# The last convolution units combined one median sooner, and four of sixteen final sums moved from VectorE to TensorE

## The chip, the cores and the metric

One core of a Trainium2 chip runs the kernel; the metric is its device time in microseconds, as the median of several executions. The engines are TensorE (PE, matrix products; its weight loads are PEld), VectorE (DVE), ScalarE (ACT), GpSimd (POOL) and SyncE (SP), which here issues every transfer.

## The reference

The input is 16 images of 128 channels by 32x32 pixels, float32. Only the end of the computation is touched by the change:

```python
y = conv3x3(concat([rimg0, rimg1], axis=1), convW_w) + convW_b      # 256 -> 128 channels
x = relu(batchnorm(y, bnW_gamma, bnW_beta))                         # statistics over all 16 images
m = median_blur(x, 3)                                               # 3x3 median, zero padding
out = x + einsum('bchw,oc->bohw', m, W) + b                         # W: 128x128
```

`rimg0` and `rimg1` come from Haar wavelet transforms of the input, the first through a 1x1 convolution, a batch norm and a ReLU (BN1). The second batch norm (BN3 in the code) needs sums over all images, so nothing of `x` exists before the last image of `y` does. Scaling by a positive factor and ReLU keep an order, so the kernel takes the medians of `y` itself, and applies scale, shift and ReLU to the median afterwards.

## The kernel before, in words

Channels lie on the 128 partitions. The 3x3 convolution runs over 20 units (`UNITS`): each image is one unit, except images 0, 1, 14 and 15, which are two units of half the rows. Units 16 and 17 are image 14, units 18 and 19 image 15. A unit u uses one of two PSUM buffers, `conv_ps[:, u % 2]`, of two banks. TensorE makes its products P and Q there (`pq`, lines 398 to 410); ScalarE copies P out (`keep_p`, line 562); VectorE puts P+Q and P-Q into the banks (`seed_even`, `seed_odd`, lines 745 to 757); TensorE adds the other taps (`outputs`, line 412); ScalarE copies the result to `y` and sums it and its squares (`keep_y`, lines 564 to 576).

TensorE's program is `outputs(u-2)`, `pq(u)`, one unit after the other, and last `outputs(19)`. `outputs(u)` waits for `seeded`, which VectorE gives when it has combined P and Q of u.

VectorE's program is one list of median pieces (`PIECES`, one for each unit; `median`, line 759), 18 instructions each. Inside the piece of unit u it combines unit u+2: early, behind line 827, or late, around line 842. The pieces of units 18 and 19 run through `step_and_more`, which counts instructions and puts others between them: BN3's fifteen small ones behind the 8th (`BN3_AT`), and one `finish(n)` behind each of the 15th to 28th (`FINISH_AT`).

Once BN3 is there, the last stage runs. ScalarE applies scale, shift and ReLU to the median of each image (`norm_median`, line 618). GpSimd zeroes its corner pixels (line 349) and maps `y` to scale*y + shift + bias (`map_x1`, line 340) for three images of four, ScalarE for the fourth (line 621). TensorE multiplies the median by W (`mix`, line 463) into `conv_ps[:, n % 2]`, and waits for `finish(n-2)`, since that reads the same buffer. VectorE's `finish(n)` (line 914) forms out = max(mapped, bias) + mix in one instruction, and SyncE sends it. Image 15 is finished and sent in two halves. Between the convolution and the mixes TensorE runs 24 products of zeros (`KEEP_WARM`, line 477).

Of the kernel before, what the change touches and what calls it, by code (L numbers as in the profile page):

```python
# [5 lines left out]
def wavelet_conv_median_kernel(nc, x, w1_t, w3_t, w2_t, vectors, out):  # L6
# [26 lines left out]
    LOW = -1.0e30  # L33
    PAIRS = IMAGES // 2
    R_HALF, X_HALF = 0, 1
    WARM_UP, KEEP_WARM = 8, 24
    RING = 8


# [25 lines left out]
    with ctx:  # L65
        def sb(name, shape, dt=fp32):
            return ctx.enter_context(nc.sbuf_tensor(name, shape, dt))
# [23 lines left out]
        v1 = sb("v1", [CH, 2 * KY * CH])  # L91
        w1 = sb("w1", [CH, CH])
        w2 = sb("w2", [CH, CH])
        p_kept = [sb(f"p_kept{k}", [CH, BANK]) for k in range(2)]
        sorted_cols = sb("sorted_cols", [CH, 3 * COLS])
        col_lo, col_mid, col_hi = (sorted_cols[:, k * COLS:(k + 1) * COLS] for k in range(3))
# [84 lines left out]
        warm = sem("warm")  # L181
        med_ready = sem("med_ready")
        mix_done = sem("mix_done")
        out_ready = sem("out_ready")
        out_sent = sem("out_sent")

# [4 lines left out]
        def zslot(n):  # L191
            return z[:, n, :]
# [31 lines left out]
        @block.sync  # L224
        def _(sp):
            sp.dma_start(w1[:, :], w1_t).then_inc(w1_in, 16)
            w3_cols = w3_t.rearrange("c t o -> c (t o)")
            for n in range(RING):
                sp.dma_start(ring[n][:, :], x_img[:, n, :]).then_inc(x_in[n], 16)
            sp.dma_start(vec[:, :], vectors).then_inc(vec_in, 16)  # L230
            for half in (X_HALF, R_HALF):
                cols = slice(half * KY * KX * CH, (half + 1) * KY * KX * CH)
                sp.dma_start(wt[:, cols], w3_cols[:, cols]).then_inc(w3_in[half], 16)
            for n in range(RING, IMAGES):
                sp.wait_ge(x_in[n - RING], 16)
                wait_xu12(sp, n - RING)
                sp.dma_start(ring[n - RING][:, :], x_img[:, n, :]).then_inc(x_in[n - RING], 16)
            sp.dma_start(w2[:, :], w2_t).then_inc(w2_in, 16)

            for n in range(IMAGES):  # L240
                if n < 2:
                    sp.wait_ge(x_in[n], 32)
                    wait_xu12(sp, n + RING)
                else:
                    sp.wait_ge(raw_in[n % 2], 16 * (n // 2))
                    sp.wait_ge(xu03_made, n - 1)
                    sp.wait_ge(x_edges_made, n - 1)
                sp.dma_start(raw[n % 2][:, :], x_img[:, n, :]).then_inc(raw_in[n % 2], 16)
            for n in range(IMAGES - 1):
                sp.wait_ge(out_ready, n + 1)  # L250
                sp.dma_start(out_img[:, n, :], slot(n)).then_inc(out_sent, 16)
            for part in range(2):
                sp.wait_ge(out_ready, IMAGES + part)
                half = slice(part * HALF, (part + 1) * HALF)
                sp.dma_start(out_img[:, IMAGES - 1, half], slot(IMAGES - 1)[:, half]).then_inc(out_sent, 16)
            sp.wait_ge(out_sent, 16 * (IMAGES + 1))

        @block.gpsimd
        def _(pool):
# [68 lines left out]
            for n in range(2, IMAGES):  # L328
# [18 lines left out]
            for n in range(1, IMAGES):  # L347
                pool.wait_ge(med_normed, n)
                G.memset(at(zslot(n), 0, [[(H - 1) * W, 2], [W - 1, 2]]), 0.0).then_inc(med_ready, 1)  # L349
                if n % 4 < 4 - ACT_SHARE:  # L350
                    map_x1(n)

        @block.tensor
        def _(pe):
# [121 lines left out]
            for _ in range(KEEP_WARM):  # L476
                nc.tensor.matmul(conv_ps[:, other, 0:BANK], zeros[:, 0:CH], zeros[:, :], start=True, stop=True)
            pe.wait_ge(w2_in, 16)
            pe.wait_ge(squares_summed, PARTS_ALL)
            for n in range(2):  # L480
                mix(n, n)
            for n in range(2, IMAGES):
                pe.wait_ge(out_ready, n - 1)
                mix(n, n % 2)

        @block.scalar
        def _(act):
# [132 lines left out]
            def map_x1(n):  # L620
                S.activation(slot(n), slot(n), ACT.Identity, bias=shift3_bias2[:, :], scale=scale3[:, :]).then_inc(x1_by_act, 1)

            for n in range(1, 4):
                norm_median(n)
            for n in range(4 - ACT_SHARE, 4):
                map_x1(n)
            for n in range(4, IMAGES):
                norm_median(n)
                if n % 4 >= 4 - ACT_SHARE:
                    map_x1(n)  # L630

        @block.vector
        def _(dve):
# [125 lines left out]
            def median(n, kept, pair0=0, pairs=BH, step=step, seeds=None):  # L759

                early, late = (seeds, None) if n in HALVED or n + 2 in HALVED else (None, seeds)
# [92 lines left out]
                PIECES.append((n, done_pairs, upto - done_pairs, u))  # L854
                done_pairs = upto

            def medians(pieces, step=step, seeds=None):
                for n, pair0, pairs, u in pieces:
                    ins = median(n, 2 * (u + 1), pair0, pairs, step, seeds)
# [13 lines left out]
            dve.wait_ge(pads_set, 1)  # L873

            dve.wait_ge(pre_kept, len(PRE))
            for u in range(len(UNITS) - 2):
                medians(PIECES[u:u + 1], seeds=u + 2)

            def second_batch_norm():
                dve.wait_ge(squares_summed, PARTS_ALL)  # L880
# [23 lines left out]
                V.scalar_tensor_tensor(shift3_bias2[:, :], mid3[:, :], neg_scale3[:, :], beta_bias2[:, :], ALU.mult, ALU.add).then_inc(bn3_ready, 1)  # L904

            def finish(n, first=0, count=PIX, part=0):
                g, k = divmod(n, 4)
                if k >= 4 - ACT_SHARE:
                    dve.wait_ge(x1_by_act, g * ACT_SHARE + k + 1 - (4 - ACT_SHARE))
                else:  # L910
                    dve.wait_ge(x1_by_pool, g * (4 - ACT_SHARE) + k + 1)
# [5 lines left out]
            for n, instruction in enumerate(FINISH_AT):  # L917
                place[instruction] = lambda n=n: finish(n)
            done = [0]

# [10 lines left out]
            for n in range(len(FINISH_AT), IMAGES - 1):  # L931
# [31 lines left out]
```

## Time and profile before

| | us |
|---|---|
| median of 3 runs (lowest, highest) | 419.66 (417.89, 421.17) |
| profiled execution, its own time | 418.86 |
| its span, first to last instruction | 417.1 |
| TensorE busy | 396.9 (95%) |
| VectorE busy | 375.6 (90%) |
| ScalarE / GpSimd busy | 152.9 / 190.8 |
| mean granted TensorE clock | 0.98 of full speed |

The span is the time between the first and the last instruction of the profiled execution; its own time has 1.76 us more around it. Starts in the rows below are counted from the start of the span. A row's length is that of the instruction, and neighbours on one engine overlap by some hundredths of a microsecond.

### The profile page before, as it was taken

What the parts mean: (1) busy time and instruction counts of PE and PEld (TensorE: products, weight loads), DVE (VectorE), ACT (ScalarE), POOL (GpSimd) and SP (SyncE); (2) the same over time, 40 slices, a digit from 0 to 9 for tenths busy, and PEclk for the clock granted to TensorE, in tenths of its full rate; (3) what the DMA queues carried; (4) which work ended last, traced back from release to release, by engine and by line L of the source; (5) the groups of instructions that cost most, each with busy time, mean ns of one, the idle gap of its engine ahead of it and who ended that gap; (6) DMA issues with size and microseconds to landing.
All of it is one profiled execution on the core that took longest, in us unless ns stands there. A gap on an engine that the chain in (4) does not pass through costs nothing.

```text
span 417.1 us, 3651 instructions
## 1 busy us (share of the span) xinstructions
PE 396.9 (95%) x1120; PEld 210.5 (50%) x1120; DVE 375.6 (90%) x532; ACT 152.9 (37%) x348; POOL 190.8 (46%) x194
## 2 busy tenths in 40 slices
PE   7889999999999999999999999999999998699983
PEld 2335588856444444444444444444446787564331
DVE  3899857999849999999999998989989999999993
ACT  2565753412262432323241414141424222229902
POOL 3999395622624443445454343434343520006620
PEclk9999999999999999999999999999999999889995
DMA  8970200100101011010101001010100000002673
GB/s 301 410 320 3 95 6 2 50 0 2 51 0 50 4 47 52 0 50 0 50 2 51 27 23 50 3 50 0 51 0 2 0 1 2 0 0 116 282 282 127
DMA packets 7796, 26.72 MB, mean 64 GB/s; under 512 B 992, under 2 KB 1248, under 8 KB 7776
## 3 DMA queue, kind: packets, MB, share of 16 engines
q1 hardware_dynamic: 7776, 26.48, 16.7%
q8 instruction: 9, 0.15, 0.1%
q14 instruction: 11, 0.09, 0.1%
HBM read 18.09 MB, written 8.39 MB: 63 GB/s over the span
## 4 chain that ended last, share of the span: by engine, by line
PE 71%; DVE 13%; POOL 5%; ACT 5%; issue 3%; DMA 2%; SPq 0%; POOLq 0%; DVEq 0%
PE conv_ps L381 65%; ACT z L618 3%; PE one_ps L363 3%; PE one_ps L446 2%; POOL y L212 2%; POOL y L213 2%; DMA ru<-x 2%; PE conv_ps L469 1%; POOL y L340 1%; DVE one_ps L821 1%; DVE sorted_cols L792 1%; DVE sorted_cols L794 1%; DVE sorted_cols L790 1%; DVE sorted_cols L787 1%; DVE z L823 1%
## 5 line engine op out<-in xcount | busy, mean ns | idle before, releaser
L381 PE MATMUL conv_ps<-ru,wt 128*128 128x512 f32 (+1 forms) x360 | 133.7, 509 | 0.0
L381 PEld LDWEIGHTS conv_ps<-ru,wt 128*128 128x128 f32 x360 | 69.9, 195 | 53.9 <-issue 50.2
L381 PE MATMUL conv_ps<-xu,wt 128*128 128x496 f32 (+3 forms) x240 | 88.6, 506 | 5.6 <-DVE conv_ps L757 5.6
L569 ACT ACTIVATE y<-conv_ps,sgn 128x512 f32<-128x512 f32 (+1 forms) x40 | 25.5, 637 | 171.0 <-PE conv_ps L381 171.0
L381 PEld LDWEIGHTS conv_ps<-xu,wt 128*128 128x128 f32 x240 | 46.0, 193 | 42.0 <-issue 33.2
L319 POOL TENSOR_TENSOR ru<-eo 128x512 f32<-128x512 f32 x16 | 17.0, 1061 | 86.5 <-DVE one_ps L785 86.4
L219 POOL TENSOR_TENSOR ru<-z 128x512 f32<-128x512 f32 x14 | 18.1, 1290 | 59.4 <-DVE one_ps L827 59.4
L381 PE MATMUL conv_ps<-ru,v 128*128 128x496 f32 (+3 forms) x120 | 43.7, 500 | 0.0
L381 PE MATMUL conv_ps<-y,wt 128*128 128x496 f32 (+3 forms) x108 | 38.6, 491 | 0.0
L381 PE MATMUL conv_ps<-y,v 128*128 128x496 f32 (+3 forms) x108 | 38.6, 491 | 0.0
L469 PE MATMUL conv_ps<-z,w 128*128 128x512 f32 x64 | 31.2, 637 | 4.8 <-POOL z L349 4.3
L363 PE MATMUL one_ps<-y,w 128*128 128x512 f32 x64 | 30.4, 605 | 4.9 <-DVE z L661 2.6
L533 ACT ACTIVATE z<-z,bn 128x256 f32<-128x256 f32 x64 | 33.0, 589 | 1.2 <-DVE bn L726 1.2
L381 PEld LDWEIGHTS conv_ps<-ru,v 128*128 128x128 f32 x120 | 22.8, 190 | 18.0 <-issue 16.8
L381 PEld LDWEIGHTS conv_ps<-y,v 128*128 128x128 f32 x108 | 20.5, 190 | 16.2 <-issue 15.3
L381 PEld LDWEIGHTS conv_ps<-y,wt 128*128 128x128 f32 x108 | 20.5, 190 | 16.2 <-issue 15.3
L562 ACT ACTIVATE p_kept<-conv_ps 128x512 f32<-128x512 f32 (+1 forms) x20 | 10.2, 512 | 48.0 <-PE conv_ps L381 48.0
L784 DVE TENSOR_TENSOR one_ps<-y 128x512 f32<-128x512 f32 (+2 forms) x20 | 11.8, 588 | 17.3 <-ACT y L569 17.3
L575 ACT ACTIVATE conv_ps<-conv_ps,neg_shift,sgn 128x512 f32<-128x512 f32 (+1 forms) x40 | 26.3, 657 | 0.0
L311 POOL TENSOR_TENSOR eo<-ru 128x512 f32<-128x512 f32 x16 | 20.7, 1292 | 8.3 <-DVE ru L741 7.1
L914 DVE SCALAR_TENSOR_TENSOR y<-y,vec,conv_ps 128x1024 f32<-128x1024 f32 (+1 forms) x17 | 20.6, 1211 | 3.9 <-PE conv_ps L469 3.9
L469 PEld LDWEIGHTS conv_ps<-z,w 128*128 128x128 f32 x64 | 11.6, 197 | 23.2 <-DVE y L914 14.1
(128 smaller groups left out, 639.8 us busy)
## 6 DMA issues: line engine op xcount, KB each, us to landing
raw<-x SPq DMA_DIRECT2D x20, 512.0 KB, 3.3
out<-y SPq DMA_DIRECT2D x15, 512.0 KB, 2.6
ru<-x SPq DMA_DIRECT2D x8, 512.0 KB, 8.7
xu<-x SPq DMA_DIRECT2D x4, 512.0 KB, 8.7
wt<-w_t SPq DMA_DIRECT2D x2, 576.0 KB, 10.6
out<-y SPq DMA_DIRECT2D x2, 256.0 KB, 2.1
w<-w_t SPq DMA_DIRECT2D x2, 64.0 KB, 4.7
vec<-vectors SPq DMA_DIRECT2D x1, 3.0 KB, 9.5
```

The source lines that it names most:

```text
L219: v.tensor_tensor(even_rows(ru12[n % 2][:, :]), a_v, h_d, ALU.add)
L311: G.tensor_tensor(even, u1, u2, ALU.add)
L319: G.tensor_tensor(at(ru03[k][:, :], 0, [[BW, H], [1, BW]]), left, odd, ALU.subtract)
L363: mm = nc.tensor.matmul(one_ps[:, n % 2, b * BANK:(b + 1) * BANK], w1[:, :], slot(n)[:, b * BANK:(b + 1) * BANK], start=True, stop=True)
L381: return nc.tensor.matmul(bank(u, b)[:, (r0 - row) * BW:(r1 - row) * BW], taps(half, kx, ky), plane[:, (r0 + dy) * BW:(r1 + dy) * BW], sta ...
L469: mm = nc.tensor.matmul(conv_ps[:, k, b * BANK:(b + 1) * BANK], w2[:, :], zslot(n)[:, b * BANK:(b + 1) * BANK], start=True, stop=True)
L533: ins = S.activation(band, band, ACT.Relu, bias=bn1[:, 5, b:b + 1], scale=bn1[:, 4, b:b + 1])
L569: S.activation(at(slot(n), row * W + b, [[2, cols]]), src, ACT.Identity, scale=sgn[:, :], accum_out=y_sum[:, part:part + 1]).then_inc(y_ke ...
L575: S.activation(src, src, ACT.Square, bias=neg_shift[:, :], scale=sgn[:, :], accum_out=y_sq[:, part:part + 1]).then_inc(squares_summed, 1)
L618: S.activation(zslot(n), zslot(n), ACT.Relu, bias=shift3[:, :], scale=scale3[:, :]).then_inc(med_normed, 1)
L784: step(V.tensor_tensor(sorted_rows(0), even, odd, ALU.min))
L914: V.scalar_tensor_tensor(v, v, cb2, conv_ps[:, n % 2, first:first + count], ALU.max, ALU.add).then_inc(out_ready, 1)
```

## The change

Six things are changed.

1. VectorE combines unit 18 late in the piece of unit 15 (image 13), where unit 17 is combined early, and unit 19 early in the piece of unit 16. Before, these stood in the pieces of units 16 and 17. The piece of unit 17 has no combining left.
2. The piece of unit 17 goes through `step_and_more` too. BN3 stands behind the 7th counted instruction of that piece; nine finishes follow the 16th, 19th, ... 40th counted instruction, and so lie in the pieces of units 18 and 19. The others follow the last median.
3. Four images (3, 6, 9, 12: `SUMMED`) have no `finish` on VectorE. ScalarE makes relu(scale*y + shift); TensorE adds it to the mix in PSUM by a product with a unit matrix; ScalarE copies the sum out with the bias.
4. `map_x1` for the other twelve images (`OWN`) is all GpSimd's.
5. GpSimd makes the unit matrix, a memset and an `affine_select`, behind its last convolution work.
6. `KEEP_WARM` goes from 24 to 30.

```diff
-    WARM_UP, KEEP_WARM = 8, 24
+    WARM_UP, KEEP_WARM = 8, 30
-    BN3_AT, FINISH_AT = 8, tuple(range(15, 29))
-    ACT_SHARE = 1
+    SUMMED = (3, 6, 9, 12)
+    OWN = [n for n in range(IMAGES) if n not in SUMMED]
+    BN3_AT, FINISH_AT = 7, (16, 19, 22, 25, 28, 31, 34, 37, 40)
...
+            G.memset(unit[:, :], 1.0).then_inc(ones_set, 1)
+            pool.wait_ge(ones_set, 1)
+            G.affine_select(out=unit[:, :], in_=unit[:, :], pattern=[[-1, CH]], base=0, channel_multiplier=1,
+                            compare_op=ALU.is_equal, fill=0.0).then_inc(unit_made, 1)
...
-                    mm = nc.tensor.matmul(conv_ps[:, k, b * BANK:(b + 1) * BANK], w2[:, :], zslot(n)[:, b * BANK:(b + 1) * BANK],
-                                          start=True, stop=True)
+                    half = slice(b * BANK, (b + 1) * BANK)
+                    mm = nc.tensor.matmul(conv_ps[:, k, half], w2[:, :], zslot(n)[:, half], start=True, stop=n in OWN)
+                    if n in SUMMED:
+                        pe.wait_ge(x1_by_act, SUMMED.index(n) + 1)
+                        mm = nc.tensor.matmul(conv_ps[:, k, half], unit[:, :], slot(n)[:, half], start=False, stop=True)
...
             for n in range(2, IMAGES):
-                pe.wait_ge(out_ready, n - 1)
+                if n - 2 in SUMMED:
+                    pe.wait_ge(out_by_act, SUMMED.index(n - 2) + 1)
+                else:
+                    pe.wait_ge(out_ready, OWN.index(n - 2) + 1)
                 mix(n, n % 2)
...
-            for n in range(4, IMAGES):
-                norm_median(n)
-                if n % 4 >= 4 - ACT_SHARE:
-                    map_x1(n)
+            for n in range(1, IMAGES):
+                norm_median(n)
+                if n in SUMMED:
+                    S.activation(slot(n), slot(n), ACT.Relu, bias=shift3[:, :], scale=scale3[:, :]).then_inc(x1_by_act, 1)
+                if n - 2 in SUMMED:
+                    act.wait_ge(mix_done, n - 1)
+                    S.activation(slot(n - 2), conv_ps[:, n % 2, :], ACT.Identity, bias=cb2).then_inc(out_by_act, 1)
...
+            last = len(UNITS) - 1
+            del EARLY[last - 3], EARLY[last - 2]
+            LATE[last - 4], EARLY[last - 3] = last - 1, last
...
-            medians(PIECES[-2:], step_and_more)
+            medians(PIECES[-3:], step_and_more)
```

**VectorE, where units 17 and 18 are combined.** Rows that read P and write `conv_ps` combine. In the kernel before, from the pieces of units 15 (1024 pixels) and 16 (448):

```order
L827 TENSOR_TENSOR one_ps<-sorted_cols 128x512
L751 TENSOR_TENSOR conv_ps<-p_kept,conv_ps 128x256
L757 TENSOR_TENSOR conv_ps<-p_kept,conv_ps 128x256
L832 TENSOR_TENSOR sorted_cols<-one_ps,z 128x32x32
...
L827 TENSOR_TENSOR one_ps<-sorted_cols 128x224
L751 TENSOR_TENSOR conv_ps<-p_kept,conv_ps 128x256
L757 TENSOR_TENSOR conv_ps<-p_kept,conv_ps 128x256
L832 TENSOR_TENSOR sorted_cols<-one_ps,z 128x14x32
```

The same two places in the changed kernel:

```order
L844 TENSOR_TENSOR one_ps<-sorted_cols 128x512
L769 TENSOR_TENSOR conv_ps<-p_kept,conv_ps 128x256
L775 TENSOR_TENSOR conv_ps<-p_kept,conv_ps 128x256
L849 TENSOR_TENSOR sorted_cols<-one_ps,z 128x32x32
...
L855 TENSOR_TENSOR sorted_cols<-one_ps,sorted_cols 128x32x32
L769 TENSOR_TENSOR conv_ps<-p_kept,conv_ps 128x256
L859 TENSOR_TENSOR one_ps<-one_ps,sorted_cols 128x1024
L775 TENSOR_TENSOR conv_ps<-p_kept,conv_ps 128x256
L863 TENSOR_TENSOR z<-one_ps,sorted_cols 128x1024
...
L769 TENSOR_TENSOR conv_ps<-p_kept,conv_ps 128x256
L775 TENSOR_TENSOR conv_ps<-p_kept,conv_ps 128x256
```

The 256-column pair for unit 18 now stands around the last but one instruction of unit 15's piece, and the pair in unit 16's piece is now that of unit 19.

**TensorE, from the keep-warm products to the mix of image 6.** The kernel before has 24 products of zeros and then 32 of `z` by `w` (two for each image) with nothing between them. The changed kernel:

```order
L495 MATMUL conv_ps<-zeros 128x512 x30
L485 MATMUL conv_ps<-z,w 128x512 x7
L488 MATMUL conv_ps<-y,unit 128x512
L485 MATMUL conv_ps<-z,w 128x512
L488 MATMUL conv_ps<-y,unit 128x512
L485 MATMUL conv_ps<-z,w 128x512 x5
L488 MATMUL conv_ps<-y,unit 128x512
L485 MATMUL conv_ps<-z,w 128x512
L488 MATMUL conv_ps<-y,unit 128x512
```

Each image of the four gets two more products, one behind each of its two mix products.

**ScalarE in the last stage.** The kernel before has `z` three or four times and then one `y` from `y`, over and over. The changed kernel:

```order
L636 ACTIVATE z<-z,shift,scale 128x512 x2
L640 ACTIVATE z<-z,shift,scale 128x1024 x3
L645 ACTIVATE y<-y,shift,scale 128x1024
L640 ACTIVATE z<-z,shift,scale 128x1024 x2
L648 ACTIVATE y<-conv_ps,vec 128x1024
L640 ACTIVATE z<-z,shift,scale 128x1024
L645 ACTIVATE y<-y,shift,scale 128x1024
```

The row that writes `y` from `conv_ps` is new; it stands in the queue ahead of the median norms of later images.

## Rows read from the trace of the kernel before

**Rows 1.** The page: its first line.

```profile
span 417.1 us, 3651 instructions
```

**Rows 2.** Chain of waits, 300 to 418 us: start, length (us), what.

```profile
377.58 3.40 ACT z L618 x3
...
398.33 11.05 issue
```

**Rows 3.** TensorE in order of time, 325 to 418 us: start, length, line, tiles, count [idle before].

```profile
342.35 1.51 PE L381 MATMUL conv_ps<-xu,wt 128*128 128x256 f32 x6
...
351.31 1.43 PE L381 MATMUL conv_ps<-ru,wt 128*128 128x256 f32 x6
355.04 1.73 PE L381 MATMUL conv_ps<-xu,wt 128*128 128x256 f32 x6 [2.30 <-DVE conv_ps L757]
356.56 2.71 PE L381 MATMUL conv_ps<-ru,wt 128*128 128x256 f32 x6
...
365.35 1.80 PE L381 MATMUL conv_ps<-xu,wt 128*128 128x256 f32 x6 [3.28 <-DVE conv_ps L757]
...
370.94 1.43 PE L381 MATMUL conv_ps<-ru,wt 128*128 128x256 f32 x6
372.21 5.34 PE L477 MATMUL conv_ps<-zeros 128*128 128x512 bf16 x24
377.39 3.61 PE L469 MATMUL conv_ps<-z,w 128*128 128x512 f32 x8
...
409.65 3.75 PE L469 MATMUL conv_ps<-z,w 128*128 128x512 f32 x4 [4.32 <-POOL z L349]
```

**Rows 4.** VectorE in order of time, same window and columns.

```profile
349.24 0.39 DVE L784 TENSOR_TENSOR one_ps<-y 128x224 f32<-128x224 f32 x1
...
354.24 0.42 DVE L751 TENSOR_TENSOR conv_ps<-p_kept,conv_ps 128x256 f32<-128x256 f32 x1
...
354.90 0.61 DVE L832 TENSOR_TENSOR sorted_cols<-one_ps,z 128x448 f32<-128x448 f32 x1
...
358.35 0.46 DVE L784 TENSOR_TENSOR one_ps<-y 128x288 f32<-128x288 f32 x1
...
362.48 0.76 DVE L821 TENSOR_TENSOR one_ps<-one_ps,sorted_cols 128x576 f32<-128x576 f32 x1
...
369.45 0.39 DVE L784 TENSOR_TENSOR one_ps<-y 128x224 f32<-128x224 f32 x1
...
373.56 0.20 DVE L882 TENSOR_REDUCE y_total<-y_sum 128x1 f32<-128x40 f32 x1
...
375.95 0.61 DVE L823 TENSOR_TENSOR z<-one_ps,sorted_cols 128x448 f32<-128x448 f32 x1
...
381.59 1.27 DVE L914 SCALAR_TENSOR_TENSOR y<-y,vec,conv_ps 128x1024 f32<-128x1024 f32 x1
382.78 0.46 DVE L784 TENSOR_TENSOR one_ps<-y 128x288 f32<-128x288 f32 x1
...
407.31 0.76 DVE L846 TENSOR_TENSOR z<-one_ps,sorted_cols 128x576 f32<-128x576 f32 x1
...
413.88 0.75 DVE L914 SCALAR_TENSOR_TENSOR y<-y,vec,conv_ps 128x512 f32<-128x512 f32 x1 [1.33 <-PE conv_ps L469]
```

**Rows 5.** ScalarE in order of time, same window and columns.

```profile
340.02 0.38 ACT L562 ACTIVATE p_kept<-conv_ps 128x256 f32<-128x256 f32 x1 [1.42 <-PE conv_ps L381]
...
408.11 1.24 ACT L618 ACTIVATE z<-z,shift,scale 128x1024 f32<-128x1024 f32 x1 [11.27 <-DVE z L846]
```

**Rows 6.** Busy time by stretch: columns as in the second line.

```profile
core 0: us, PE busy (x) PEld busy (x) DVE busy (x) ACT busy (x) POOL busy (x), PEclk, DMA share, GB/s
...
356.00:358.00 2.00, 2.00 (x7) 1.65 (x6) 1.93 (x5) 0.00 (x0) 0.00 (x0) 0.56 0.00 0
...
406.00:408.00 2.00, 0.00 (x0) 0.00 (x0) 1.93 (x4) 0.00 (x0) 0.00 (x0) 0.86 0.66 266
```

**Rows 7.** TensorE in order of time, 0 to 32 us, columns as in Rows 3.

```profile
6.21 4.05 PE L363 MATMUL one_ps<-y,w 128*128 128x512 f32 x8 [1.43 <-DVE y L213]
```

**Rows 8.** One line's instructions: ScalarE's copies out of PSUM, 1024 columns wide.

```profile
L583 ACT ACTIVATE y<-one_ps x2: 1018/1026/1033, 58.5 to 59.4; 128x1024 f32<-128x1024 f32 x2
```

More of the change, by code:

```diff
@@ L93, in wavelet_conv_median_kernel @@
         w2 = sb("w2", [CH, CH])
+        unit = sb("unit", [CH, CH])
         p_kept = [sb(f"p_kept{k}", [CH, BANK]) for k in range(2)]
@@ L183, in wavelet_conv_median_kernel @@
         mix_done = sem("mix_done")
+        ones_set = sem("ones_set")
+        unit_made = sem("unit_made")
+        out_by_act = sem("out_by_act")
         out_ready = sem("out_ready")
@@ L349, in _ @@
                 G.memset(at(zslot(n), 0, [[(H - 1) * W, 2], [W - 1, 2]]), 0.0).then_inc(med_ready, 1)
-                if n % 4 < 4 - ACT_SHARE:
+                if n in OWN:
                     map_x1(n)
@@ L478, in _ @@
             pe.wait_ge(w2_in, 16)
+            pe.wait_ge(unit_made, 1)
             pe.wait_ge(squares_summed, PARTS_ALL)
@@ L482, in _ @@
             for n in range(2, IMAGES):
-                pe.wait_ge(out_ready, n - 1)
+                if n - 2 in SUMMED:
+                    pe.wait_ge(out_by_act, SUMMED.index(n - 2) + 1)
+                else:
+                    pe.wait_ge(out_ready, OWN.index(n - 2) + 1)
                 mix(n, n % 2)
@@ L618, in norm_median @@
                 S.activation(zslot(n), zslot(n), ACT.Relu, bias=shift3[:, :], scale=scale3[:, :]).then_inc(med_normed, 1)
-            def map_x1(n):
-                S.activation(slot(n), slot(n), ACT.Identity, bias=shift3_bias2[:, :], scale=scale3[:, :]).then_inc(x1_by_act, 1)
-            for n in range(1, 4):
+            for n in range(1, IMAGES):
                 norm_median(n)
-            for n in range(4 - ACT_SHARE, 4):
-                map_x1(n)
-            for n in range(4, IMAGES):
-                norm_median(n)
-                if n % 4 >= 4 - ACT_SHARE:
-                    map_x1(n)
+                if n in SUMMED:
+                    S.activation(slot(n), slot(n), ACT.Relu, bias=shift3[:, :], scale=scale3[:, :]).then_inc(x1_by_act, 1)
+                if n - 2 in SUMMED:
+                    act.wait_ge(mix_done, n - 1)
+                    S.activation(slot(n - 2), conv_ps[:, n % 2, :], ACT.Identity, bias=cb2).then_inc(out_by_act, 1)
         @block.vector
@@ L757, in seed_odd, with median @@
                 V.tensor_tensor(q_bank, p_kept[u % 2][:, 0:cols], q_bank, ALU.subtract).then_inc(seeded, 1)
-            def median(n, kept, pair0=0, pairs=BH, step=step, seeds=None):
-                early, late = (seeds, None) if n in HALVED or n + 2 in HALVED else (None, seeds)
+            def median(n, kept, pair0=0, pairs=BH, step=step, early=None, late=None):
                 r0, nr = 2 * pair0, 2 * pairs
@@ L855, in _, with medians @@
                 done_pairs = upto
-            def medians(pieces, step=step, seeds=None):
+            EARLY, LATE = {}, {}
+            for u in range(2, len(UNITS)):
+                before = EARLY if UNITS[u - 2][0] in HALVED or UNITS[u][0] in HALVED else LATE
+                before[u - 2] = u
+            last = len(UNITS) - 1
+            del EARLY[last - 3], EARLY[last - 2]
+            LATE[last - 4], EARLY[last - 3] = last - 1, last
+            def medians(pieces, step=step):
                 for n, pair0, pairs, u in pieces:
-                    ins = median(n, 2 * (u + 1), pair0, pairs, step, seeds)
+                    ins = median(n, 2 * (u + 1), pair0, pairs, step, EARLY.get(u), LATE.get(u))
                     if pair0 + pairs == BH:
@@ L875, in _ @@
             dve.wait_ge(pre_kept, len(PRE))
-            for u in range(len(UNITS) - 2):
-                medians(PIECES[u:u + 1], seeds=u + 2)
+            medians(PIECES[:-3])
             def second_batch_norm():
@@ L906, in finish @@
             def finish(n, first=0, count=PIX, part=0):
[L907 to L911, printed above, removed]
+                dve.wait_ge(x1_by_pool, OWN.index(n) + 1)
                 dve.wait_ge(mix_done, n + 1 + part)
@@ L916, in _ @@
             place = {BN3_AT: second_batch_norm}
-            for n, instruction in enumerate(FINISH_AT):
+            for n, instruction in zip(OWN, FINISH_AT):
                 place[instruction] = lambda n=n: finish(n)
@@ L925, in step_and_more @@
                     place.pop(done[0])()
-            medians(PIECES[-2:], step_and_more)
+            medians(PIECES[-3:], step_and_more)
             for instruction in sorted(place):
                 place[instruction]()
-            for n in range(len(FINISH_AT), IMAGES - 1):
+            for n in OWN[len(FINISH_AT):-1]:
                 finish(n)
```

5 lines of the change are left out of this document (3 added, 2 removed).

## The prediction, made before the changed kernel ran

> **What bounds the kernel now.** I read the busy shares and the clock first, then the chain of waits from its end, and then each engine in order of time from 325 us on. The change touches nothing of weight before 341 us, so all sums lie behind that; the span is 417.1 us [rows 1].
>
> The chain ends in three stages. First the convolution: TensorE waits twice for VectorE to combine a unit, 2.30 us before unit 18's outputs at 355.04 and 3.28 us before unit 19's at 365.35 [rows 3]. In between it had nothing else to do, since VectorE combines those units only inside the pieces of units 16 and 17. Second BN3, at 373.56 on VectorE, 2.62 us behind the start of TensorE's last six products (370.94), over at 375.95 [rows 3, 4]. Third the last stage. The chain names ScalarE (3.40 us of z) and then 11.05 us of "issue" [rows 2]; that is VectorE working through medians and finishes without a gap until its last median instruction starts at 407.31 [rows 4]. What follows it is serial: ScalarE's norm of image 15 at 408.11 [rows 5], its mix at 409.65 in 3.75 us, which is half pace, since two images took 3.61 us at 377.39 [rows 3], two half finishes, the last at 413.88 [rows 4], and a transfer. So two things count: when VectorE gets through, and how fast the end runs.
>
> **Prices from these rows.** A product of zeros takes 0.216 us start to start (5.18 us for 24), and the last of a group shows 0.16 more (5.34 - 5.18) [rows 3]. So six 256-column products take 1.43 - 0.16 = 1.27 us, the 24 of one unit's outputs 5.07, and a mix instruction 512 wide (3.61 - 0.16) / 8 = 0.43; an image has four of them, 1.72 us. VectorE's rows overlap by 0.08 us (a finish is 1.27 long and takes 381.59 to 382.78, 1.19) [rows 4]. So in a piece of 448 pixels a wide instruction takes 0.53 and a narrow one 0.31, in one of 576 pixels 0.67 and 0.37. Combining a 256-column unit costs 0.66 (354.24 to 354.90). The whole piece of unit 16 takes 9.11 (349.24 to 358.35), 8.45 without combining; that of unit 17 takes 11.10 (358.35 to 369.45), 10.44 without [rows 4].
>
> **Combining sooner.** Unit 18 can be combined in the piece of unit 15: its P was copied at 340.02 and TensorE had left its products at 342.35 [rows 3, 5], and the late place comes near 346. TensorE then runs unit 17's outputs, unit 19's P and Q (last six at 351.31, done 352.58 [rows 3]) and at once unit 18's outputs, to 357.65. Unit 19 is combined at 354.24 + 0.66, so by 355.6, and its outputs follow without a wait to 362.72. The last six start at 361.45; plus 2.62 gives BN3's start, 364.07. VectorE stands at BN3's new place (behind line 819 of unit 17's piece) at 362.48 + 0.66 = 363.14 [rows 4]: it waits 0.9 us. BN3 is over at 364.07 + 2.39 = **366.46, which is 9.5 us sooner**. The two falls of the clock in this stretch (0.56 in 356 to 358 [rows 6]) go with the stalls.
>
> **What VectorE still has to do.** Nothing of the medians is removed, so most of the 9.5 us is only exchanged: 6.31 us of unit 17's piece (362.48 to 369.45, less 0.66) and all of unit 18's now follow BN3. VectorE's list from 366.46 to the start of its last median instruction is 6.31 + 8.45 + 10.44 - 0.67 = 24.5 us of medians and 9 finishes of 1.19 = 10.7. Without waits that start is 401.7, against 407.31. Five finishes left this stretch: four are gone, one moved behind it.
>
> **What TensorE adds.** Four images get four more instructions each, 1.72 us an image, priced as the mixes: same shape and type, and no row of before has one with the unit matrix. Bounds: the zeros' 0.216 and half-clock pace, 3.75/4 = 0.94 an instruction. I take 0.43, the row of its own kind. This work is not hidden:
> - The 30 products of zeros run from 362.7 to 369.2. Mixes 0 and 1 follow to 372.7. Finish 0 comes when VectorE has done 6.31 and one narrow instruction, 373.1 to 374.3, so mix 2 starts at 374.4 (a gap of 1.7). Finish 1 follows 1.9 us of median, 376.2 to 377.4; mix 3 starts at 377.5 (a gap of 1.4).
> - From there TensorE is full: mixes 3 to 10 with the sums of 3, 6 and 9 are eleven times 1.72, 18.9 us, to 396.4. VectorE waits for it at finish 4 (1.8 us), at 7 (0.8) and at 10 (0.7), 3.3 us in all. These three waits take the place of those removed.
> - Finish 10 starts at 396.6. Behind it come 1.19, three median instructions (1.7), finish 11 (1.19) and eight more (5.0): the last median instruction starts at 396.6 + 9.1 - 0.67 = **405.0**, 2.3 us sooner than before.
>
> **What ScalarE and GpSimd take.** In each group of three images ScalarE has three norms, a ReLU and a copy out of PSUM. A norm is 1.24 long (about 1.15 to the next) [rows 5], a copy out of PSUM 1.03 [rows 8]; at most 5 x 1.24 = 6.2 us against TensorE's 6.9. The copy waits for a mix and stands ahead of the norm that the mix after the next one needs: TensorE meanwhile has two mixes, 3.4 us, against 0.2 + 1.15 + 1.15 + 0.2 = 2.7 for copy, norm and zeroing. Slack 0.7, so nothing. GpSimd has at most two maps in a row and keeps ahead; the unit matrix is made while it idles between 340 and 376 us. SyncE sends in order of images, and image 3 is ready before 4.
>
> **The end.** From the start of the last median instruction to mix 15 it is 409.65 - 407.31 = 2.34 us, so mix 15 starts at 407.4. To the end of the span it is then 417.1 - 409.65 = 7.4 us at half clock, giving 414.8; at full clock the mix takes 3.61 - 4 x 0.43 = 1.9 instead of 3.75, giving 412.9. Before, TensorE had idled 4.32 us and the clock fell while it was idle (0.86 in 406 to 408) [rows 3, 6]. Now it idles about 2.2. The nearest row is the idle of 2.30, after which the first six products ran at 1.73 and the next six at 2.71 [rows 3]: the clock fell more than a microsecond after the restart. So I take the middle, **413.9**, and keep both ends.
>
> **The sum.** 413.9 + 1.76 (418.86 less 417.1) = 415.7, against 418.86: 3.2 us less, of which 2.3 is VectorE's and 0.9 the clock's. The median of the runs, 419.66, stands 0.8 above the profiled one, so by it 416.5. I say **416.0**.
>
> **The clock, row against rule.** The changed kernel has two gaps of 1.7 and 1.4 us around mix 2, where before TensorE was full. The nearest rows: a wait of 1.43 us at 6.21, behind which eight 512-column instructions took 4.05 us, full pace [rows 7], and the 2.30 that was followed by half pace [rows 3]. I take it to hold, and keep one fall as a rival. The Trainium skill ("TensorE: Matmul & The Clock Gate", "A second HAM failure mode: psum-queue depth-cycling") says that a TensorE which idles briefly between groups while it cycles through PSUM buffers goes back and forth between its two clocks; that speaks against this change. By that rule the saving would shrink or turn; the row at 6.21, two PSUM buffers in turn too, doesn't show it.
>
> **Rivals.**
> 1. *One fall of the clock around mixes 2 to 4.* For: two gaps close together. Against: rows 7. A stall's fall lasted about 3.5 us (four slow microseconds at 0.56 [rows 6]), costs 1.7 us of work, and TensorE is full behind it, so it passes through: 416.0 + 1.7 = 417.7. Chance 0.17.
> 2. *TensorE is not the limit* (the unit products are cheaper, as the zeros' 0.216 would make them, or the waits fall elsewhere). VectorE's waits shrink to 1.5 us and the saving grows by 1.8: 414.2. Chance 0.12.
> 3. *Slower: the clock goes back and forth through the last stage.* TensorE is full from 377.5 to 396.4, so each microsecond at 1.2 GHz costs half of one there. The saving of 3.2 is gone at 6.4 us of half clock, and 1% slower (4.2 us) needs 14.8 us of it. All of it at half clock would give 433. For: the rule above. Against: a full TensorE was always back at 2.4 GHz some 3.5 us after a fall. At 15 us: 420.2. Chance 0.05.
> 4. *The time doesn't move*: ScalarE's queue has no slack (its 0.7 us used up by copies that wait longer), which costs a few times 0.7 us, or the transfers of images 13 to 15, now closer together, end last. 418.5. Chance 0.06.
>
> **How the numbers follow.** The forecast has 0.60; its own range is 415.0 (full clock at the end, by the median) to 417.3 (half clock). Taking in rivals 1 and 2 and the spread of the runs, 413.8 to 418.6. This kernel can't tell under 1%, 4.2 us, from no change. The forecast's full-clock end is at the edge of that, so I give faster 0.28 (rival 2 and a quarter of the forecast), same 0.67, slower 0.05.
>
> **What would show it.** BN3 starts near 364 with a wait of about 0.9 us for ScalarE; TensorE has no wait between 343 and 369; VectorE waits for mixes at three finishes, some 3 us in all; last median instruction near 405; mix 15 between 1.9 and 3.75 us. Wrong if VectorE's waits pass 5 us, if the unit products take other than 0.43 each, or if the clock is below full between 370 and 405.

## The result and the profile after

The changed kernel takes 416.83 us in the median of 20 runs (415.65 to 418.56), the kernel before 419.51 (20 runs). The ratio is 0.9947, 95% interval 0.9934 to 0.996: 2.2 us faster, between 1.7 and 2.8. The two medians differ by 2.7. The profiled execution took 416.90 us, its span is 415.1.

TensorE through the end of the convolution and the last stage, in order of time (start, length, line, tiles, count, idle before); these answer to [rows 3]:

```profile
351.30 1.43 PE L396 MATMUL conv_ps<-ru,wt 128*128 128x256 f32 x6
352.57 1.43 PE L396 MATMUL conv_ps<-xu,wt 128*128 128x256 f32 x6
...
361.45 1.43 PE L396 MATMUL conv_ps<-ru,wt 128*128 128x256 f32 x6
362.72 6.64 PE L495 MATMUL conv_ps<-zeros 128*128 128x512 bf16 x30
369.19 3.60 PE L485 MATMUL conv_ps<-z,w 128*128 128x512 f32 x8
374.40 1.98 PE L485 MATMUL conv_ps<-z,w 128*128 128x512 f32 x4 [1.61 <-DVE y L935]
378.15 1.12 PE L485 MATMUL conv_ps<-z,w 128*128 128x512 f32 x2 [1.76 <-DVE y L935]
379.11 1.02 PE L488 MATMUL conv_ps<-y,unit 128*128 128x512 f32 x2
...
402.29 3.60 PE L485 MATMUL conv_ps<-z,w 128*128 128x512 f32 x8
408.16 3.65 PE L485 MATMUL conv_ps<-z,w 128*128 128x512 f32 x4 [2.28 <-POOL z L364]
```

The two stalls of the convolution (2.30 and 3.28 us before) are gone. The unit products (line 488) run at the pace of the mixes. From 378.15 to 405.9 TensorE has no idle; mix 15, the last row, runs at half pace.

VectorE, same columns, against [rows 4]:

```profile
362.50 0.46 DVE L836 TENSOR_TENSOR one_ps<-sorted_cols 128x288 f32<-128x288 f32 x1
364.06 0.20 DVE L907 TENSOR_REDUCE y_total<-y_sum 128x1 f32<-128x40 f32 x1 [1.10 <-ACT conv_ps L597]
...
373.07 1.28 DVE L935 SCALAR_TENSOR_TENSOR y<-y,vec,conv_ps 128x1024 f32<-128x1024 f32 x1
374.26 1.05 DVE L802 TENSOR_TENSOR one_ps<-y 128x224 f32<-128x224 f32 x1
375.23 0.61 DVE L804 TENSOR_TENSOR sorted_cols<-one_ps,y 128x448 f32<-128x448 f32 x1
...
383.68 1.28 DVE L935 SCALAR_TENSOR_TENSOR y<-y,vec,conv_ps 128x1024 f32<-128x1024 f32 x1 [1.88 <-PE conv_ps L485]
...
390.54 1.28 DVE L935 SCALAR_TENSOR_TENSOR y<-y,vec,conv_ps 128x1024 f32<-128x1024 f32 x1 [0.64 <-PE conv_ps L485]
...
397.41 1.28 DVE L935 SCALAR_TENSOR_TENSOR y<-y,vec,conv_ps 128x1024 f32<-128x1024 f32 x1 [0.62 <-PE conv_ps L485]
...
405.82 0.76 DVE L863 TENSOR_TENSOR z<-one_ps,sorted_cols 128x576 f32<-128x576 f32 x1
```

BN3 starts at 364.06, 9.5 us sooner. VectorE then waits for mixes three times, 3.14 us in all, where before it hardly waited ahead of image 15. The last median instruction starts at 405.82, only 1.5 us sooner than before. One row has no counterpart in the forecast: line 802 at 374.26 takes 1.05 us; its neighbour of the same size, line 801 at 372.77, takes 0.39. Both are narrow median instructions, which have half as many columns (224 or 288) as their piece has pixels.

The chain of waits, from 376 us (start, length, what), against [rows 2]:

```profile
376.91 1.20 DVE y L935
378.11 0.04 issue
378.15 1.12 PE conv_ps L485 x2
```

It runs from finish 1 straight into TensorE and stays there to 395.60, where before it named ScalarE and "issue". Behind that it goes over ScalarE and GpSimd, and ends with 4.67 us of "issue" before mix 15, in which VectorE works through its last medians. The clock that TensorE was granted, by stretch (busy time of PE, PEld, DVE, ACT, POOL, then the granted clock as a share of full speed, DMA share, GB/s), against [rows 6]:

```profile
343.00:369.00 26.00, 26.00 (x125) 20.52 (x124) 24.57 (x56) 9.70 (x29) 0.96 (x3) 1.00 0.00 1
370.00:405.00 35.00, 31.62 (x74) 13.43 (x73) 31.71 (x47) 22.90 (x21) 13.05 (x23) 1.00 0.46 187
...
408.00:412.00 4.00, 3.65 (x4) 1.08 (x4) 1.78 (x3) 0.00 (x0) 1.19 (x2) 0.57 0.69 277
```

Full clock up to 405 us, in spite of the two gaps around mix 2; 0.57 for mix 15.

In the experiments everything up to BN3 shifts by up to 3 us from one profiled execution to another, so I cut each span in three: up to BN3's start (first part), from there to the start of the last median instruction (second part), and from there to the end (third part). The column "first products" tells how fast TensorE's first products of data ran, at some 6 us: most of their weight loads are 0.43 us apart (full pace) or 0.86 (half).

| kernel | BN3 starts | to last median instruction | to the end | span | first products |
|---|---|---|---|---|---|
| before | 373.56 | 33.75 | 9.8 | 417.1 | full |
| changed | 364.06 | 41.76 | 9.3 | 415.1 | full |
| sooner only | 365.46 | 45.01 | 9.7 | 420.2 | half |
| sums only | 375.68 | 32.83 | 11.0 | 419.5 | half |
| no unit products | 364.60 | 40.16 | 8.3 | 413.1 | full |
| late zeros | 366.56 | 41.76 | 8.2 | 416.5 | half |
| fewer zeros | 365.50 | 41.78 | 8.6 | 415.9 | half |
| placed, sums at 2, 5, 8, 11 | 363.92 | 38.50 | 8.3 | 410.7 | full |
| placed, sums as changed | 363.92 | 38.53 | 8.5 | 411.0 | full |
| three sums | 365.26 | 39.91 | 8.2 | 413.4 | half |
| map 4 on ScalarE | 364.25 | 41.09 | 9.2 | 414.5 | full |
| placed, maps 9 and 13 on ScalarE | 366.81 | 37.29 | 8.2 | 412.3 | half |

So the change is 9.5 us off the first part, 8.0 back in the second, 0.5 off the third. The shift up to BN3 goes with the column at the right: among the ten kernels with the early BN3 it starts at 363.92 to 364.60 where the first products ran at full pace, and at 365.26 to 366.81 where they ran at half. All twelve profiles have the same gap there, of 1.26 to 2.24 us, and its length doesn't sort them (1.37 to 1.64 full, 1.26 to 2.24 half).

### The profile page after: what moved, and what is told of

It is laid out like the page before. It is cut to its first block, busy times and chain, and to the rows that moved or that the text cites. A ratio compares the mean times of both kernels' runs of the same rounds, so it can differ in the third digit from the quotient of the medians.

```text
span 415.1 us, 3695 instructions
## 1 busy us (share of the span) xinstructions
PE 400.2 (96%) x1142; PEld 212.9 (51%) x1142; DVE 371.9 (90%) x528; ACT 157.3 (38%) x352; POOL 192.5 (46%) x196
## 4 chain that ended last, share of the span: by engine, by line
PE 86%; POOL 5%; DVE 3%; issue 2%; DMA 2%; ACT 1%; SPq 0%; POOLq 0%; DVEq 0%
PE conv_ps L396 76%; PE conv_ps L485 4%; PE one_ps L378 3%; PE one_ps L461 2%; POOL y L219 2%; POOL y L220 2%; DMA ru<-x 2%; PE conv_ps L488 1%; DVE y L935 1%; POOL y L355 1%; ACT z L640 1%; SPq L236 0%; ACT y L645 0%; ACT y L648 0%; POOL v L285 0%
## 5 line engine op out<-in xcount | busy, mean ns | idle before, releaser
L396 PE MATMUL conv_ps<-ru,wt 128*128 128x512 f32 (+1 forms) x360 | 131.2, 501 | 0.0
L396 PEld LDWEIGHTS conv_ps<-ru,wt 128*128 128x128 f32 x360 | 68.4, 190 | 53.1 <-issue 50.1
L396 PE MATMUL conv_ps<-xu,wt 128*128 128x496 f32 (+3 forms) x240 | 87.5, 501 | 0.0
L378 PEld LDWEIGHTS one_ps<-y,w 128*128 128x128 f32 x64 | 11.2, 190 | 21.0 <-issue 17.4
```

The costliest lines, as they stand in the source:

```text
L378: mm = nc.tensor.matmul(one_ps[:, n % 2, b * BANK:(b + 1) * BANK], w1[:, :], slot(n)[:, b * BANK:(b + 1) * BANK], start=True, stop=True)
L396: return nc.tensor.matmul(bank(u, b)[:, (r0 - row) * BW:(r1 - row) * BW], taps(half, kx, ky), plane[:, (r0 + dy) * BW:(r1 + dy) * BW], sta ...
```

## The experiments

The edits are against the changed kernel. Ratios are against the kernel before, run on the same chip in the same rounds.

**1. The combining sooner, without the sums.**

```diff
-    SUMMED = (3, 6, 9, 12)
+    SUMMED = ()
+    ACT_MAPPED = (3, 7, 11, 15)
...
-    BN3_AT, FINISH_AT = 7, (16, 19, 22, 25, 28, 31, 34, 37, 40)
+    BN3_AT, FINISH_AT = 7, tuple(range(16, 43, 2))
...
```

> The combining one median sooner and BN3 in the piece of unit 17 stay; the four sums go back: all sixteen images are finished on VectorE (14 finishes, one behind every second counted instruction from the 16th), maps as in the kernel before. Theory 'two limits' (behind BN3 the later of VectorE's and TensorE's lists sets the end; VectorE was full before, so an earlier BN3 alone gives it nothing): last median instruction starts at 366.5 + 24.5 + 14 x 1.19 + some 0.7 = 408.4, against 407.31 before; time the same as before or up to 1.5 us more, 418.9 to 421. Rival 'the earlier BN3 is the gain': all or more of the changed kernel's gain stays, 2 us or more under the kernel before.

Measured: 421.06 us, ratio 1.0033 (1.0014 to 1.0052), 1.4 us slower. BN3 is about as early as in the changed kernel, and VectorE then needs 45.0 us (44.3 forecast): no wait for a mix anywhere before image 15, only work. The rival falls: an earlier BN3 gives a full VectorE nothing. The loss has two sources. One is the 1.10 us that VectorE waits for BN3's sums. The other is two narrow median instructions:

```profile
375.67 1.06 DVE L805 TENSOR_TENSOR one_ps<-y 128x224 f32<-128x224 f32 x1
...
381.15 1.24 DVE L837 TENSOR_TENSOR one_ps<-sorted_cols 128x224 f32<-128x224 f32 x1
```

They take 1.5 us more than two of 0.39; the kernel before has only 0.27 us of this, at one instruction. Experiment 9 is about the cause. By these rows the second source is 1.2 us, as large as the first; without it the earlier BN3 alone would come out about even. That is an estimate, no run shows it.

**2. The sums, without combining sooner.**

```diff
-            last = len(UNITS) - 1
-            del EARLY[last - 3], EARLY[last - 2]
-            LATE[last - 4], EARLY[last - 3] = last - 1, last
...
-    BN3_AT, FINISH_AT = 7, (16, 19, 22, 25, 28, 31, 34, 37, 40)
+    BN3_AT, FINISH_AT = 8, tuple(range(15, 32, 2))
...
-            medians(PIECES[-3:], step_and_more)
+            medians(PIECES[-2:], step_and_more)
```

> The four sums on TensorE and ScalarE stay; the combining and BN3 go back to their old places, 24 products of zeros, nine finishes behind the 15th, 17th, ... 31st counted instruction of the last two pieces. Theory 'two limits': TensorE's list starts at 377.4 and is 19 x 1.72 = 32.7 us up to mix 15 with no wait, so mix 15 can't start before 410.1 (409.65 before), but at full clock since TensorE never idles: mix 15 takes 1.9 instead of 3.75. Last median instruction near 406.6. Time within 1 us of the kernel before, 0 to 1 less. Rival 'four finishes fewer on VectorE are the gain': 2 to 4 us under the kernel before.

Measured: 421.49 us, ratio 1.0037 (1.0014 to 1.006), 1.6 us slower, outside my 0 to 1 us less. The rival falls: four finishes fewer on VectorE gain nothing by themselves. The second part is near the forecast (32.83; 33.0 forecast; VectorE waits 7.6 us in it and behind it in four waits of 1.35 to 2.32), and mix 15 runs at full clock without an idle before it, but 37.3 us behind BN3's start, 0.8 later than forecast. The rest of the miss is ahead of BN3, in TensorE's rows:

```profile
366.44 2.88 PE L396 MATMUL conv_ps<-xu,wt 128*128 128x256 f32 x6 [4.97 <-DVE conv_ps L775]
369.11 2.71 PE L396 MATMUL conv_ps<-ru,wt 128*128 128x256 f32 x6
371.61 1.62 PE L396 MATMUL conv_ps<-xu,wt 128*128 128x256 f32 x6
373.07 1.43 PE L396 MATMUL conv_ps<-ru,wt 128*128 128x256 f32 x6
```

Here unit 18's outputs ran at full clock, behind the same idle of 2.30 us that was followed by half clock in the kernel before. So TensorE idled 4.97 us, and unit 19's outputs ran at half clock from the start: 6.6 us from their first row to the last six, against 5.6 before. That is 1.0 us of BN3's 2.1; the other 1.1 stands in this profile before unit 18's outputs already (356.13 against 355.04) and goes with its slower first products. With the old combining, BN3's start hangs on when the clock falls. Neither half gains alone; each costs about 1.5 us. The whole gains 2.2.

**3. The unit products left out** (images 3, 6, 9 and 12 lack their first summand).

```diff
-                        mm = nc.tensor.matmul(conv_ps[:, k, half], unit[:, :], slot(n)[:, half], start=False, stop=True)
```

> The changed kernel without the 8 products by the unit matrix (images 3, 6, 9, 12 lack their first summand); waits, copies and order stay. Theory 'two limits': TensorE's list gets 6.9 us shorter, VectorE's waits at finishes 4, 7 and 10 shrink from 3.1 us to about 1.5 or less, the last median instruction starts near 404 instead of 405.8, time 1.5 to 2 us under the changed kernel. Rival 'VectorE waits for something else (ScalarE's copy, GpSimd's map)': the waits and the time stay within 0.5 us of the changed kernel.

Measured: 414.85 us, ratio 0.9881 (0.9854 to 0.9908), 2.0 us under the changed kernel by the medians. VectorE's three waits are 0.79, 0.30 and 0.46, 1.55 us in all instead of 3.14. So TensorE's list, with the products in it, makes half of the waits, and the rival falls; the products cost 1.6 us of the second part. The 1.55 us that are left have another cause, and it is VectorE's own: mixes 4, 7 and 10 start 0.17 to 0.18 us behind the ends of finishes 2, 5 and 8, whose PSUM buffers they need, and finishes 4, 7 and 10 stand too soon behind these for a mix to fit in.

**4. Seven products of zeros ahead of mix 14.**

```diff
+                if n == IMAGES - 2:
+                    for _ in range(7):
+                        nc.tensor.matmul(conv_ps[:, 0, 0:BANK], zeros[:, 0:CH], zeros[:, :], start=True, stop=True)
                 mix(n, n % 2)
```

> The changed kernel with 7 products of zeros (1.5 us) between the mixes of images 13 and 14, into the buffer that mix 14 then overwrites. They shorten TensorE's idle before mix 15 from 2.28 to about 0.8 us and shift no finish. Theory 'the end hangs on the clock': mix 15 takes 1.9 us instead of 3.65 wherever the clock had fallen, so the runs lose their slower half: median 0.7 to 1.5 us under the changed kernel. Rival 'mix 15 is long for another reason, or the transfers set the end': no change within 0.3 us, or 0.3 slower.

Measured: 416.35 us, ratio 0.9925 (0.9895 to 0.9955). TensorE's last row:

```profile
410.66 1.96 PE L485 MATMUL conv_ps<-z,w 128*128 128x512 f32 x4 [0.77 <-POOL z L364]
```

The idle is 0.77 and mix 15 takes 1.96, as forecast; the third part is 8.2 instead of 9.3. The gain by the medians, 0.5 us, is under my 0.7 to 1.5, and the ratio alone doesn't separate the two kernels. The changed kernel's own runs say more: nine of its twenty have a mean granted clock of 0.999 or more, and their median is 416.55; the other eleven have 0.990 to 0.996, and 417.9. Only the profiled one of them shows where its clock was low. But the kernels that idle under 2 us before mix 15 (late zeros, both placed ones, three sums, and experiment 10) have 0.998 or more in all of their 30 runs. So I take the half-clock end to cost 1.1 us (third part) to 1.3 (medians of the two groups), and to fall in about half of the runs.

**5 and 6. Other places for the finishes, with and without other images summed.**

```diff
-    WARM_UP, KEEP_WARM = 8, 30
+    WARM_UP, KEEP_WARM = 8, 24
...
-    SUMMED = (3, 6, 9, 12)
+    SUMMED = (2, 5, 8, 11)
...
-    BN3_AT, FINISH_AT = 7, (16, 19, 22, 25, 28, 31, 34, 37, 40)
+    BN3_AT, FINISH_AT = 7, (14, 16, 22, 25, 30, 32, 38, 39, 45)
```

This is experiment 5. In experiment 6 `SUMMED` stays at (3, 6, 9, 12), and the places are 14, 16, 22, 26, 28, 33, 35, 41, 43.

> The changed kernel with the sums at images 2, 5, 8, 11, finishes behind the 14th, 16th, 22nd, 25th, 30th, 32nd, 38th, 39th and 45th counted instruction, and 24 products of zeros. Theory 'two limits': TensorE starts its list 1.3 us sooner, idles less around mix 2 and is ahead where VectorE used to wait for it, so the 3.1 us of VectorE's waits vanish; last median instruction starts near 402.4 for a BN3 at 364.1 (38.4 us behind BN3's start, 41.8 in the changed kernel), TensorE idles about 1 us before mix 15, which runs at full clock. Span near 410 to 411, time 3 to 5 us under the changed kernel. Rival 'VectorE's waits move elsewhere' (to ScalarE's copies or GpSimd's maps): under 1 us.

> As the run before it in this list, but the sums stay at images 3, 6, 9, 12; finishes behind the 14th, 16th, 22nd, 26th, 28th, 33rd, 35th, 41st and 43rd. Tells the places of the finishes from the choice of images. Theory: the places do it; last median instruction 38.6 us behind BN3's start, no idle of over 0.5 us before mix 15, time 3 to 5 us under the changed kernel, within 1 us of the run before.

Measured: 413.5 us, ratio 0.984 (0.9813 to 0.9866), and 413.6 us, 0.9845 (0.9817 to 0.9873): 1.6% under the kernel before, over 3 us under the changed one, and alike. VectorE has no wait for a mix before image 15 in the first and one of 0.29, behind the last median, in the second. The places do it, not the choice of images. Both have 24 products of zeros instead of 30; that isn't it either, since with 24 and the places of the changed kernel (experiment 7) the second part stays at 41.78. Of experiment 5, TensorE:

```profile
372.36 1.13 PE L485 MATMUL conv_ps<-z,w 128*128 128x512 f32 x2 [0.74 <-DVE y L935]
...
404.76 1.96 PE L485 MATMUL conv_ps<-z,w 128*128 128x512 f32 x4 [1.01 <-POOL z L364]
```

Mix 2 starts 2.0 us sooner than in the changed kernel and the idle before mix 15 is 1.01, with full clock.

**7. Fewer products of zeros.**

```diff
-    WARM_UP, KEEP_WARM = 8, 30
+    WARM_UP, KEEP_WARM = 8, 24
```

> The changed kernel with 24 instead of 30 products of zeros. Mixes 0 and 1 run 1.3 us sooner, and TensorE idles about 2.9 us before mix 2 instead of 1.6, then 1.8 before mix 3. Theory 'the zeros only keep the clock': if the clock falls around mixes 2 to 4, TensorE's list ends 1 to 1.7 us later and the time is 1 to 2 us over the changed kernel; no finish and no mix from 2 on moves otherwise. Rival 'the zeros do nothing here': within 0.4 us.

Measured: 417.7 us, ratio 0.9932 (0.99 to 0.9965), not to be told from the changed kernel: neither theory shows in the time. Its trace is worth more:

```profile
375.83 3.39 PE L485 MATMUL conv_ps<-z,w 128*128 128x512 f32 x4 [2.64 <-DVE y L935]
379.58 1.16 PE L485 MATMUL conv_ps<-z,w 128*128 128x512 f32 x2 [0.36 <-DVE y L935]
```

The clock did fall (0.57 from 376 to 380): mix 2 took 3.39 instead of 1.98. But it was done 0.36 us before mix 3 could start, since that waits for finish 1 anyway, and the second part is 41.78 against 41.76. My price for such a fall, 1.7 us, was wrong here: where TensorE has slack, half clock costs nothing. A fall behind mix 3, where TensorE has no slack, stands in no trace, so its price is untested.

**8. Three sums.**

```diff
-    WARM_UP, KEEP_WARM = 8, 30
+    WARM_UP, KEEP_WARM = 8, 24
...
-    SUMMED = (3, 6, 9, 12)
+    SUMMED = (3, 7, 11)
...
-    BN3_AT, FINISH_AT = 7, (16, 19, 22, 25, 28, 31, 34, 37, 40)
+    BN3_AT, FINISH_AT = 7, (13, 16, 19, 26, 27, 31, 34, 36, 40, 44)
```

> Three sums (images 3, 7, 11), ten finishes behind the 13th, 16th, 19th, 26th, 27th, 31st, 34th, 36th, 40th and 44th, 24 products of zeros. Against four sums VectorE has 1.19 us more, TensorE 1.72 less. Theory 'two limits': once the waits are gone VectorE's list is the longer one, so the last median instruction starts 1.2 us later than with four sums (39.6 us behind BN3's start), TensorE idles 1.8 us before mix 15: 1.2 us over the four-sum version with its places, more where the clock falls at the end, still 1 to 3 under the changed kernel.

Measured: 414.63 us, ratio 0.9872 (0.9845 to 0.99); second part 39.91 (39.6 forecast) against 38.50, and by the medians 1.1 us over experiment 5. VectorE has no wait for a mix before image 15, and TensorE idles 1.81 us before mix 15 (1.8 forecast). With the places right VectorE's list is the longer one, and a fourth sum is worth a finish.

**9. The map of image 4 on ScalarE.** In the changed kernel line 802 is slow while GpSimd runs this map (GpSimd, same columns):

```profile
373.88 1.20 POOL L355 TENSOR_SCALAR y<-y,scale,shift_bias 128x1024 f32<-128x1024 f32 x1
375.01 0.10 POOL L364 MEMSET z<- 128x4 f32 x1
```

```diff
+    MAPPED_BY_ACT = (4,)
+    BEHIND_NORM = {5: 4}
...
-                if n in OWN:
+                if n in OWN and n not in MAPPED_BY_ACT:
                     map_x1(n)
...
+                if n in BEHIND_NORM:
+                    m = BEHIND_NORM[n]
+                    S.activation(slot(m), slot(m), ACT.Identity, bias=shift3_bias2[:, :], scale=scale3[:, :]).then_inc(own_by_act, 1)
...
```

> The changed kernel with the map of image 4 made by ScalarE (idle there for 7 us) instead of GpSimd; everything else stays. In the changed kernel the narrow median instruction of line 802 behind the first finish took 1.05 us instead of 0.39, and GpSimd's map of image 4 ran over its start and ended 0.3 us before it did. Theory 'port': a VectorE instruction with both inputs in SBUF does not run beside a GpSimd map and waits for it. Then line 802 takes 0.39, finish 1 and mix 3 come 0.66 us sooner, and since TensorE is full from mix 3 on, all of it goes through: 0.5 to 0.7 us under the changed kernel. Rival 'the first finish or the first output transfer slows it': line 802 stays at 1.05, time unchanged.

Measured: 416.29 us, ratio 0.9923 (0.9893 to 0.9952); the interval is too wide for 0.6 us, the trace is not. VectorE behind the first finish:

```profile
373.25 1.27 DVE L944 SCALAR_TENSOR_TENSOR y<-y,vec,conv_ps 128x1024 f32<-128x1024 f32 x1
374.44 0.39 DVE L808 TENSOR_TENSOR one_ps<-y 128x224 f32<-128x224 f32 x1
```

The same instruction (line 808 here) takes 0.39, right behind the same finish; the second part is 41.09, 0.67 shorter. The first finish and the first output transfer are where they were, so the rival falls.

**10. The version of experiment 5 with two maps on ScalarE.** The first two lines differ from experiment 5; the rest of the edit is that of experiment 9.

```diff
+    MAPPED_BY_ACT = (9, 13)
+    BEHIND_NORM = {10: 9, 13: 13}
```

> The version with the sums at images 2, 5, 8, 11 and the new places, with the maps of images 9 and 13 made by ScalarE. In that version two narrow median instructions took 1.07 and 1.06 instead of 0.46, each over a GpSimd map (of images 9 and 13). Theory 'port': both fall to 0.46, the last median instruction starts 37.3 us behind BN3's start instead of 38.5, time 0.6 to 1.2 us under that version (TensorE has only about 1 us to give). Rival: no change.

Measured: 412.48 us, ratio 0.9829 (0.9798 to 0.9859), the lowest of all, though its interval overlaps that of experiment 5. Two VectorE rows of experiment 5, and the answering two of this one:

```profile
388.35 1.07 DVE L802 TENSOR_TENSOR one_ps<-y 128x288 f32<-128x288 f32 x1
...
396.44 1.06 DVE L842 TENSOR_TENSOR one_ps<-sorted_cols 128x288 f32<-128x288 f32 x1
```

```profile
391.24 0.46 DVE L808 TENSOR_TENSOR one_ps<-y 128x288 f32<-128x288 f32 x1
...
398.72 0.46 DVE L848 TENSOR_TENSOR one_ps<-sorted_cols 128x288 f32<-128x288 f32 x1
```

Both at 0.46, and the second part is 37.29, as forecast.

## Why the prediction was right, and where it was not

**Combining sooner.** Right: BN3 was put at 364.07 and started at 364.06, with no wait of TensorE in between and both falls of the clock gone. That it fits to 0.01 us is luck: other profiles with the same combining have BN3 anywhere from 363.92 to 366.81. That goes with the pace of TensorE's first products, and the two profiles that were compared both had them at full pace.

**Most of it is only exchanged.** Right, and shown by experiment 1: with all finishes back on VectorE the 9.5 us gives nothing, and the kernel is slower.

**TensorE becomes the limit.** Right: the unit products run at a mix's 0.43 us, VectorE waits at finishes 4, 7 and 10 for 1.88, 0.64 and 0.62 us (1.8, 0.8 and 0.7 forecast), and experiment 3 takes half of that away by taking the products away. The other half hangs on where the finishes stand, which the prediction took as given. That neither part gains alone I had not put in these words; experiments 1 and 2 show it.

**The last median instruction** was put at 405.0 and started at 405.82. This term was too small by 0.8 us. I had priced every narrow instruction at its usual length, with "GpSimd keeps ahead" as all that GpSimd could do to VectorE. Line 802 took 0.66 more; experiment 9 gives it back. Since TensorE waits for finish 1 and is full from there on, all of it went through. The other 0.17 us lie behind mix 3's start: finish 10 starts 19.26 us behind it, 19.1 forecast.

**The end.** I took the middle between a mix 15 of 1.9 and one of 3.75 us. The profiled one took 3.65, behind an idle of 2.28, so the span of 415.1 is the 413.9 of the forecast, 0.8 from the term above, and most of a microsecond of clock, less 0.4 for two half finishes that followed closer than before (the wait of the last fell from 1.33 to 0.95 us). Over the runs the middle seems right: nine of twenty have a mean clock of 0.999 or more (experiment 4).

**The sum.** 3.2 us forecast, 2.2 measured by the ratio and 2.7 by the medians (416.83 measured, 416.0 said).

**The clock, row against rule.** The two gaps of 1.61 and 1.76 us left it at full in the profiled run, so the trace doesn't show the going back and forth; with a gap of 2.64 it fell once (experiment 7), and even that was hidden. But the row that the prediction set against the rule, full pace behind 1.43 us at 6.21, was one of two outcomes: in six of the twelve profiles the products at this place ran at half pace, behind gaps from 1.26 to 2.24 us. One trace made it look firmer than it is, and that the clock held around mix 2 doesn't make it firm.

**The rivals.** Rival 1 failed on its price in the one place where a fall was seen, mix 2. Rival 2's cheaper products were not there; its time, 414.2, is near what leaving them out gives (414.85). Of rival 4, ScalarE's queue had its slack: it idles 1.23 us before each of the later three copies out of PSUM. The transfers didn't end later either: from the last half finish's end to the end of the span it is 2.4 us, 2.5 before.

**Sums that don't come out.** In rival 3, 15 us at half clock cost 7.5 and lead from 416.0 to 423.5, not 420.2, and all 18.9 us at half clock lead to 434.9, not 433. The forecast's lower end by the median is 412.9 + 1.76 + 0.8 = 415.5, not 415.0, if it is worked out as the upper one was. None of this touches the 416.0.

## What to carry to other kernels

When an engine is full, taking its wait for another engine away, or starting its stage sooner, moves work and gains nothing; it gains only together with work taken off it, and then only as far as the engine that receives the work has room *at the times when it is asked*. Write both lists with their start times, and place the steps by which one waits for the other so that neither does: here that was worth more than the change itself (by the medians 3.3 us against 2.7, by the ratios 4.5 against 2.2). Read single slow instructions against their neighbours of the same size, and look what runs beside them. And before a single row is used as evidence of a habit of the chip, look for the same place in other profiles.

## What the runs showed of the hardware

**VectorE beside GpSimd.** In these traces a VectorE instruction with both inputs in SBUF does not run beside GpSimd's map, whose input and output are in SBUF, and waits for its end. Line 802 at 374.26 ended at 375.31, 0.23 us behind the end of the map at 373.88; the wide ones, which read PSUM and SBUF, keep their length beside maps, as do the finishes, which read both as well. It was there in the kernel before too, once: line 817 at 392.28 took 0.73 instead of 0.46. Experiment 1 has it twice (1.06 and 1.24 instead of 0.39), experiment 6 once (1.20 instead of 0.46). It works the other way as well, GpSimd's row for a map beside the narrow pair at 401.5 in the changed kernel:

```profile
401.47 1.75 POOL L355 TENSOR_SCALAR y<-y,scale,shift_bias 128x1024 f32<-128x1024 f32 x1
```

It takes 1.75 instead of 1.20; the two rows start within 0.03 us, too close to tell which was first. The Trainium skill says so ("SBUF — State Buffer", "🔬 SBUF: two separate sides"): a VectorE instruction with two SBUF inputs and a GpSimd one take turns on one pair of ports, each for its whole length. The traces agree, and experiments 9 and 10 show it by moving the maps.

**TensorE's clock at mix 15.** The idle before mix 15, and how long mix 15 took, in all profiles but that of experiment 2, which has no idle there: 0.21, 0.77, 1.01 (twice) and 1.81 us, and 1.95 to 1.96 each time, full pace; 2.28 us three times, and 3.65, 3.57 and 3.00; 2.80 us, and 2.68; 4.32 and 5.73 us, and 3.75 both times, half pace throughout. So the length of the idle alone doesn't fix how long the half pace lasts, and the kernel before and experiment 2 differ likewise behind one and the same idle of 2.30 us.

**TensorE's pace at the start.** In every profile the eight products of zeros that open the kernel take 3.35 to 3.60 us, some 0.42 each, against 0.22 each in the stretch before the mixes: half pace. The products of data that follow at some 6 us ran at full pace in six profiles and most of them at half in the other six. The changed kernel and late zeros, behind almost the same idle:

```profile
6.48 3.93 PE L378 MATMUL one_ps<-y,w 128*128 128x512 f32 x8 [1.64 <-DVE y L220]
...
6.54 8.46 PE L378 MATMUL one_ps<-y,w 128*128 128x512 f32 x12 [1.70 <-DVE y L220]
```

In four of the six slower ones (late zeros, sums only, three sums, experiment 10) the granted clock nevertheless reads 1.00 there; it is the distance of the weight loads, 0.86 instead of 0.43 us, that gives the pace away.
